# A decoder layer on one core: four steps split in parts, and a new order of steps on every engine

## The reference

```python
x = x + attn(layernorm(x))          # 4 heads
x = x + xattn(layernorm(x), ctx)    # 16 heads, context [32, 77, 256], masked
x = x + ffn(layernorm(x))           # 8 experts of width 64, the best 2 of each token
# attn: q, k, v = silu(short_conv(h @ Wq | Wk | Wv)), 4 taps; rope(q), rope(k)
#   s = clip(h @ Ws, -32, 32); z = cumlogsumexp(s); g = exp(z_prev - z); s_norm = exp(s - z)
#   hk = hk * g + k s_norm;  ok = q hk;  qv = softmax(ok)
#   hv = hv * g + s_norm v;  ov = qv hv
#   attn = (ov * rsqrt(mean(ov * ov) + eps) * gnorm * silu(h @ Wg)) @ Wo
# xattn: softmax(Q K^T / 4 + mask) V @ W_proj + b
# ffn: w = softmax(top2(h @ gate)); s = silu(h @ Wu) * (h @ Wv); sum over the 2 of w (s @ Wo)
```

## Time and profile before

| | |
|---|---|
| median of 3 runs | 1521.48 us (1519.7 to 1524.4) |
| the profiled execution | 1518.72 us, its span 1516.6 us |
| busy in the span | PE 96%, PEld 85%, DVE 80%, ACT 63%, POOL 55% |
| chain that ended last | PE 91%, DVE 3%, the rest 1 to 2% each |
| granted TensorE clock | 0.989 of full speed as a mean |
| DMA | 45.03 MB, mean 30 GB/s |

### The profile page before, as it was taken

How to read it: one execution, slowest core, us unless ns; L and a number is a source line. 1 busy time by engine, 2 the same in 40 slices (tenths; PEclk the granted TensorE clock), 3 DMA queues, 4 the chain that set the end, 5 groups by cost and what they waited for, 6 DMA issues and landing times.

```text
span 1516.6 us, 31405 instructions
## 1 busy us (share of the span) xinstructions
PE 1456.9 (96%) x10520; PEld 1291.4 (85%) x10520; DVE 1217.1 (80%) x3006; ACT 961.4 (63%) x2531; POOL 828.6 (55%) x937
## 2 busy tenths in 40 slices
...
DMA packets 113102, 45.03 MB, mean 30 GB/s; under 512 B 86192, under 2 KB 109104, under 8 KB 112944
## 3 DMA queue, kind: packets, MB, share of 16 engines
...
...
## 4 chain that ended last, share of the span: by engine, by line
PE 91%; DVE 3%; issue 2%; POOL 1%; ACT 1%; DMA 1%; SPq 0%; POOLq 0%; DVEq 0%; ACTq 0%
PE bank L444 76%; PE bank L450 7%; PE bank L685 5%; PE bank L770 2%; PE bank L532 1%; DVE a_conv L887 1%; PE bank L738 0%; DVE a_rC L909 0%; ACT x_prob L1331 0%; SPq L433 0%; DMA x_prob<-in_ctxT 0%; DVE x_nmax L1013 0%; DMA x<-in_x 0%; PE bank L541 0%; DVE x L1035 0%
## 5 line engine op out<-in xcount | busy, mean ns | idle before, releaser
L1331 ACT ACTIVATE x_prob<-bank,x_nmax 128x77 f32<-128x77 f32 x1024 | 248.5, 329 | 51.2 <-DVE x_nmax L1013 50.2
L1013 DVE TENSOR_REDUCE x_nmax<-bank 128x4 f32<-128x308 f32 x256 | 120.1, 469 | 109.8 <-PE bank L444 106.0
L1344 ACT ACTIVATE x_probT<-bank 128x256 f32<-128x256 f32 (+1 forms) x256 | 112.2, 438 | 98.3 <-PE bank L685 98.1
L1497 POOL TENSOR_TENSOR a_orinv<-a_ove,mhalf 128x8 f32<-128x8 f32 x32 | 65.1, 2035 | 199.1 <-DVE a_ove L952 199.1
L444 PE MATMUL bank<-x_Vbd,x_probT 128*128 128x34 f32 (+1 forms) x1280 | 162.5, 267 | 0.7 <-DVE x_o L1027 0.7
L887 DVE SCALAR_TENSOR_TENSOR a_conv<-a_raw,cw,a_conv 128x256 f32<-128x256 f32 x384 | 155.0, 478 | 7.5 <-POOL a_conv L1459 7.5
L444 PEld LDWEIGHTS bank<-x_Vbd,x_probT 128*128 128x128 f32 x1280 | 158.0, 192 | 1.1 <-DVE x_o L1027 1.1
L685 PE MATMUL bank<-ident,x_prob 128*128 128x128 f32 x640 | 114.6, 277 | 0.4 <-ACT x_prob L1331 0.3
L909 DVE RECIPROCAL a_rC<-bank 128x512 f32<-128x512 f32 x32 | 107.1, 3348 | 0.6 <-PE bank L444 0.6
L912 DVE TENSOR_TENSOR a_AT<-bank,tri 128x512 f32<-128x512 f32 x128 | 87.7, 685 | 23.9 <-PE bank L444 23.9
L444 PE MATMUL bank<-x_K_bd,x_Q_stack 128*128 128x308 f32 x256 | 94.5, 369 | 8.6 <-ACT x_prob L1331 5.2
...
## 6 DMA issues: line engine op xcount, KB each, us to landing
...
x_Vbd<-v_tok SPq DMA_DIRECT2D x128, 9.6 KB
```

What stands on the lines that cost most here:

```text
L1013: dve.tensor_reduce(nmax[:, u % 2, :], X0[:, 0:UH * S2].rearrange("p (h s) -> p h s", h=UH), AX.X, ALU.min).then_inc(on.x_max, 1)
L1331: ins = act.activation(prob[:, col:col + S2], X0[:, i * S2:(i + 1) * S2], ACT.Exp, scale=-1.0, bias=nmax[:, u % 2, i:i + 1])
L1344: act.activation(probT[:, g[0]:g[-1] + 1, :].rearrange("p h t -> p (h t)"), X1[:, 0:len(g) * P], ACT.Copy).then_inc(on.x_pT, 1)
```

## The change

The step a_conv becomes six parts a_conv(i, h) of two instructions each, a_rc two parts of 128x256, x_kbd six parts of one instruction, f_yy two. x_kbd's part 0 runs at the end of the body before (as an A step), x_proj at the start of the body after (as an F step), a_et and a_qbd on ACT at the end of the body of their own row. In SP's list x_kin comes one iteration later, x_vbd one earlier, and the load of x ahead of the last store. Every engine's list has a new order. Below, the old lists are left out (they stand in the listing above).

```diff
                 if r > 1:
-                    sp.wait_ge(on.x_kbd, upto(r - 2))
+                    sp.wait_ge(on.x_kbd, upto(r - 2, QU + KC))
...
-                N(g_store, 0); N(g_store, 1); N(x_load); N(g_store, 2); N(g_store, 3); L(a_load); A(x_vbd)
-                F(f_store); N(x_kin)
+                N(g_store, 0); A(x_load); A(x_kin); N(g_store, 1); N(g_store, 2); L(a_load); N(g_store, 3)
+                F(f_store); N(x_vbd)
...
-                pe.wait_ge(on.a_rC, upto(r))
+                pe.wait_ge(on.a_rC, upto(r, TC))
...
-                    pe.wait_ge(on.x_kbd, upto(r))
+                    pe.wait_ge(on.x_kbd, upto(r, QU + KC))
...
-            def f_yy(r):
+            def f_yy(r, c):
                 pe.wait_ge(on.f_sT, upto(r, TC))
                 pe.wait_ge(on.f_sTl, upto(r, TC))
                 pe.wait_ge(on.f_s, upto(r, TC))
-                for c in range(TC):
-                    ins = mm_halves(F0[:, c * D:(c + 1) * D], [
-                        (lambda h, i=i: fsT[h][:, c, i, :], lambda h, i=i: fwo[h][:, i, :]) for i in range(RC)])
-                ins.then_inc(on.f_y_ps, 1)
+                mm_halves(F0[:, c * D:(c + 1) * D], [
+                    (lambda h, i=i: fsT[h][:, c, i, :], lambda h, i=i: fwo[h][:, i, :]) for i in range(RC)]
...
+                A(a_ktok); F(x_proj); A(a_A, 0); A(a_vtok); N(g_mm, 0); N(g_mm, 1); X(x_turn); A(a_A, 1)
+                A(a_state); X(x_q); N(g_mm, 2); N(a_turn); F(f_turn); A(a_ok); N(a_qk); X(x_s, 0); N(g_mm, 3)
+                F(f_gate); F(f_u0); X(x_s, 1); N(a_v); X(x_pt, 0); F(f_lg); N(g_mm, 4); X(x_s, 2); A(a_qt)
+                F(f_v0); N(a_s); X(x_pt, 1); X(x_s, 3); X(x_av, 0); A(a_P, 0); A(a_P, 1); X(x_s, 4)
+                X(x_pt, 2); X(x_av, 1); A(a_o); N(g_mm, 5); X(x_pt, 3); X(x_av, 2); X(x_s, 5); N(a_g)
+                F(f_st, 0); F(f_u1); N(g_mm, 6); X(x_s, 6); X(x_av, 3); F(f_v1); X(x_s, 7); X(x_pt, 4); N(a_c)
+                X(x_pt, 5); A(a_ot); X(x_av, 4); X(x_pt, 6); X(x_av, 5); X(x_pt, 7); N(g_mm, 7); F(f_st, 1)
+                X(x_av, 6); X(x_av, 7); N(a_et); A(a_wo); F(f_yy, 0); X(x_ot); F(f_yy, 1)
...
-            def a_conv(r):
+            def a_conv(r, i, h):
 
                 dve.wait_ge(on.a_tap0, upto(r))
-                n = 0
-                for i in range(1, TAPS):
-                    for j in range(4):
-                        n += 1
-                        if i > 1:
-                            dve.wait_ge(on.a_conv, upto(r, 3 * 4, n - 4))
-                        stt(conv[:, j, :], raw[:, j, i:i + T], cw[:, j, i:i + 1], conv[:, j, :],
-                                 ALU.mult, ALU.add).then_inc(on.a_conv, 1)
+                for j in (2 * h, 2 * h + 1):
+                    n = 4 * (i - 1) + j + 1
+                    if i > 1:
+                        dve.wait_ge(on.a_conv, upto(r, 3 * 4, n - 4))
+                    stt(conv[:, j, :], raw[:, j, i:i + T], cw[:, j, i:i + 1], conv[:, j, :],
+                        ALU.mult, ALU.add).then_inc(on.a_conv, 1)
 
             def a_silu_qk(r):
...
-            def a_rc(r):
+            def a_rc(r, c):
                 dve.wait_ge(on.a_C_ps, upto(r))
                 if r > 1:
                     dve.wait_ge(on.a_qn, upto(r - 2))
-                dve.reciprocal(flat(rC[r % 2]), E0[:, :]).then_inc(on.a_rC, 1)
+                dve.reciprocal(rC[r % 2][:, c, :], E0[:, c * D:(c + 1) * D]).then_inc(on.a_rC, 1)
 
...
-                dve.wait_ge(on.f_y_ps, upto(r))
+                dve.wait_ge(on.f_y_ps, upto(r, TC))
...
+                N(a_stats); F(x_out); N(a_mv); F(f_stats); N(a_ve); A(a_maskA, 0); F(f_mv); N(g_lo, 0)
+                F(f_ve); X(x_xntl); N(g_lo, 1); A(a_maskA, 1); A(a_state); N(a_xntl); X(x_ql); F(f_xntl)
+                A(a_okn); X(x_soft, 0); A(a_max); X(x_soft, 1); F(f_logit); A(a_sum); F(f_top); X(x_soft, 2)
+                F(f_gap); N(a_conv, 1, 0); N(a_conv, 1, 1); F(f_su, 0); F(f_gden); F(f_gw1); F(f_topf)
+                A(a_ssq); F(f_gw2); X(x_soft, 3); F(f_wt12); F(f_s, 0); A(a_maskP, 0); A(a_maskP, 1)
+                X(x_soft, 4); N(a_conv, 2, 0); N(a_conv, 2, 1); F(f_wt); N(a_conv, 3, 0); N(a_conv, 3, 1)
+                A(a_oss); X(x_soft, 5); A(a_ove); N(a_silu_qk); N(a_rot); F(f_stl, 0); X(x_soft, 6); A(a_o1)
+                X(x_rs, 0); F(f_su, 1); N(a_gate); X(x_o, 0); X(x_soft, 7); F(f_s, 1); N(g_lo, 2); N(g_lo, 3)
+                N(a_rc, 0); N(a_rc, 1); A(a_otl); F(f_stl, 1); N(a_silu_v); X(x_rs, 1); X(x_o, 1); A(a_out)
+                A(x_stats); A(x_mv); X(x_otl); A(x_ve); F(f_out)
...
+                N(g_out, 0); A(a_ktok); A(a_vtok); N(g_out, 1); X(x_xnt); N(a_xn); F(f_xn); X(x_q); N(a_xnt)
+                F(f_xnt); N(a_raw_qk); F(f_lgt); N(g_out, 2); X(x_prob, 0); N(g_out, 3); A(a_oke)
+                X(x_prob, 1); N(a_raw_v); F(f_th, 0); X(x_pt, 0); X(x_prob, 2); F(f_gap); A(a_qnt); X(x_pt, 1)
+                N(a_e); N(g_out, 4); X(x_prob, 3); X(x_pt, 2); X(x_prob, 4); A(a_osq); N(a_convt, 0)
+                X(x_pt, 3); X(x_prob, 5); F(f_st, 0); N(a_ehi); N(a_gt); F(f_th, 1); X(x_prob, 6); X(x_pt, 4)
+                X(x_prob, 7); X(x_pt, 5); N(g_out, 5); A(a_ot); N(g_out, 6); X(x_pt, 6); N(a_convt, 1)
+                X(x_pt, 7); F(f_st, 1); X(x_ot); N(g_out, 7); N(a_qbd); N(a_et); A(x_xn)
...
-            def x_kbd(r):
+            def x_kbd(r, m):
 
                 pool.wait_ge(k_in[r % 2], loaded(r, 3))
                 if r > 0:
                     pool.wait_ge(on.x_s_ps, upto(r - 1, NU))
-                for q in range(QU):
-                    pool.tensor_tensor(K_bd[:, q], K_stack[r % 2][:, q:q + 1, :].broadcast_to([P, UH, S2]),
-                                       spread(groupmask[:], S2), ALU.mult)
-                for f in range(KC):
-                    ins = pool.tensor_tensor(KT_lo_bd[:, f],
-                                             KT_lo[r % 2][:, f:f + 1, :].broadcast_to([P, HB, S2]),
-                                             spread(headmask[:], S2), ALU.mult)
-                ins.then_inc(on.x_kbd, 1)
+                if m < QU:
+                    pool.tensor_tensor(K_bd[:, m], K_stack[r % 2][:, m:m + 1, :].broadcast_to([P, UH, S2]),
+                                       spread(groupmask[:], S2), ALU.mult).then_inc(on.x_kbd, 1)
+                else:
+                    f = m - QU
+                    pool.tensor_tensor(KT_lo_bd[:, f], KT_lo[r % 2][:, f:f + 1, :].broadcast_to([P, HB, S2]),
+                                       spread(headmask[:], S2), ALU.mult).then_inc(on.x_kbd, 1)
 
...
+                X(x_neg); X(x_rstd); X(x_kbd, 1); X(x_kbd, 2); N(a_rstd); F(f_rstd); X(x_kbd, 3); X(x_kbd, 4)
+                X(x_kbd, 5); X(x_x1b); A(a_oks); A(a_qn); N(a_tap0); N(a_clip); F(f_sw, 0); A(a_orinv)
+                N(a_elo); A(a_o2); N(a_cos); F(f_sw, 1); N(a_sin); A(x_kbd, 0); N(a_kr)
```

More of the change, by code:

```diff
@@ L776, in f_yy @@
                 pe.wait_ge(on.f_s, upto(r, TC))
-                for c in range(TC):
-                    ins = mm_halves(F0[:, c * D:(c + 1) * D], [
-                        (lambda h, i=i: fsT[h][:, c, i, :], lambda h, i=i: fwo[h][:, i, :]) for i in range(RC)])
-                ins.then_inc(on.f_y_ps, 1)
+                mm_halves(F0[:, c * D:(c + 1) * D], [
+                    (lambda h, i=i: fsT[h][:, c, i, :], lambda h, i=i: fwo[h][:, i, :]) for i in range(RC)]
+                    ).then_inc(on.f_y_ps, 1)
             def body(rn, ra, rx, rf):
```

18 lines of the change are left out of this document (removed).

## The result

| | before | after |
|---|---|---|
| median of 4 runs | 1521.11 us | 1550.07 us (1548.18 to 1550.25) |
| ratio | | 1.0184 (95%: 1.0166 to 1.0203) |
| span of the profiled execution | 1516.6 us | 1548.0 us |

The change makes the kernel 29 us slower. I had forecast 1518.6 and a range to 1532.

The account below looks back on a forecast made before the run. It took PE's matmul stream as the bound. Steady terms +0.02 − 0.49 + 0.44 = −0.03 per iteration, × 29 = −0.9 us, with tail −3 and head +1 gave −2.9, so 1518.6 us; range 1504 to 1532.

Parts of the forecast that it names:

- What bounds the kernel: PE's matmul stream, busy in all 43.78 us of a steady iteration; 43.29 needed with nobody late.
- PE's own cost: PE: 13 places, not 11, where an f32 transpose group meets a split product; +0.02 per iteration, ends 0 and +0.2.
- Stalls removed: PE's waits at x_pt, x_av, a_ot, a_A, f_st1 and a_turn all go: −0.49 per iteration, other end 0.
- Convolution: Six parts on DVE: a late a_tap0 delays x_soft 3, a_P's masks and a_o; +0.05 per iteration, ends 0 and +0.3.
- a_conv's first part idle on a_tap0: DVE: idle time of a_conv's first part on a_tap0 would show the convolution's term.
- A port: DVE and POOL side by side, third taps by f_sw0: at most 0.6 per iteration, on engines with over 1 us slack.
- rival (c): Taps and POOL's f_sw0 exclude one another, x_soft 5 about 1.0 late, +0.4 per iteration: 1530 us; chance 0.06.
- x_proj: Behind x_ot: chain to x_proj 1.99 against cover 1.93; +0.08 per iteration, ends 0 and +0.5.
- Softmax chain: New waits per iteration: 0.07 between x_s0 and x_s1, 0.08 at x_pt6, 0.03 at x_q; ends 0 and +0.4.
- K_bd, reciprocal: K_bd in six parts: 0 in steady rows, +0.1 at worst; reciprocal in halves: nothing, without slack +0.07.
- Tail −3: Last iterations: shorter waits of x_s0, first for KT_lo_bd, and x_ot between f_yy's halves; −3 us, 0 to −5.
- Range: Whole kernel: 1504 us (stalls gone, no new ones, tail's far end) to 1532 us (x_proj 0.45 late).

Follow-up runs that it names:

- run 9: Kernel before with a_o1 moved on DVE ahead of a_gate and f_su 1: 1523.60 us, ratio 1.0024 to before.
- run 1: Changed kernel with all its split steps but every engine's list as before: 1520.23 us, ratio 0.9993 to before.
- run 10: Changed kernel with f_su 0 moved on DVE ahead of the first convolution tap, a_conv(1, 0): 1542.22 us.
- run 3: Changed kernel with a_clip moved on POOL from ahead of f_sw 0 to behind it: 1548.74 us.
- run 13: Changed kernel with f_su 0 ahead of the first tap, f_wt ahead of a_P's masks, x_ot ahead of f_yy 0, a_clip behind f_sw 0: 1528.63 us.
- Run 5: Changed kernel with x_ot moved on PE ahead of both halves of f_yy: 1542.86 us.

## Why the prediction was wrong

- *What bounds the kernel*: half right. PE was busy all the time and its starts showed 0.49 lost. But "what this matmul stream needs with nobody late" isn't what it can reach: run 9 took 0.34 of these waits away, and the period rose by 0.2.
- *PE's own cost, +0.02*: at least 0.08, at a_o, where x_av now stands ahead of it. In run 1, which has none of the new neighbours, the period was 43.88, so 0.1 is also what the same list varies by.
- *Stalls removed, −0.49*: about 0.39 went (x_pt 6, a_ot, a_A1, f_st 1). x_av 4's 0.11 came back as another wait.
- *Convolution, +0.05, ends 0 and +0.3*: **this is the step that failed, the term that was mis-sized most: 0.49 measured**, all of it ahead of a_o. I had the chain right (a_tap0, first tap, x_soft 3, masks, a_o), and its sign too (a_conv's first part idle on a_tap0), and mis-sized it. Two runs split it: DVE's idle time on a_tap0 and the work behind it, 0.19 when f_su 0 fills it (run 10), and POOL's clip on f_wt12, 0.36 (run 3); together they are a little more than the wait, and with both gone it is gone (run 13).
- *A port*: the second half of the same error. I took 0.36 in twelve taps as the price and said that over 1 us of slack lay there. The price was near for the clip (0.35 on f_wt12), but the slack was not there, and the tap beside f_sw 0 was blocked for 0.8: its longest took 1.27 instead of 0.48, as 2.45 − 1.65 for the four says too. The Trainium skill ("SBUF — State Buffer", "SBUF: two separate sides") has an exclusive lock for the whole instruction between a vector instruction with two SBUF inputs and a GpSimd instruction that reads SBUF. f_sw 0 agrees (1.04 us long, 0.8 blocked, and itself 0.11 longer). The clip doesn't: it takes 1.93, and taps beside it lose 0.08 (run 13) to 0.36 in all. My rival (c) named f_sw 0 as the mechanism; it made x_soft 5 late by 0.8, but PE was itself late by the wait ahead of a_o, so its price was 0.09 alone.
- *x_proj, +0.08*: 0.22. The chain was right: x_ot to the copy 0.64, copy 0.59, low half 0.69, in the medians. The signals were too small: the low half ends 1.96 behind x_ot's start, and x_proj starts at 2.10. With 0.14 there and 0.04 ahead of the low half they are 0.18, not 0.08. Run 5 gave 0.17 of the loss back.
- *Softmax chain, +0.18*: at least 0.43, the second largest miss. x_pt 6 and 7 are 0.33, where I had 0.08. f_gate is 0.10: it starts 0.10 behind the end of f_xntl, where it had 0.75, and f_xntl stands behind a_xntl, for which DVE idles 81.1 us in 32 rows (17.7 before). That was read from the timelines; no run moved it.
- *K_bd, reciprocal*: nothing in steady rows, as said (run 1).
- *Tail −3*: −0.15 in the first tail interval and −0.3 behind the last mark. The waits for KT_lo_bd are gone, and x_s0 comes 1.04 sooner after the mark in the interval that held the first (4.48, not 5.52), but what follows there takes 0.89 more; why was not tested. x_s0 still waits 2.0 in the next tail iteration, now for x_ql, as I had worked out:

```profile
PE bank L444 <- DVE x_Q_stack L999: 2.0, 1, 2.0
```

- *Range*: its far end allowed one of five new waits to be large (0.45). Three were: 0.49 ahead of a_o, 0.33 at x_pt 6 and 7, 0.22 at x_proj. These add up, as each goes or stays without the others (runs 5 and 13). What I named makes 0.49 + 0.33 + 0.22 + 0.10 + 0.08 − 0.39 = 0.83 of the 1.00; the rest is not told apart.
